# Four layer normalisations of an eight-block kernel: three dissolved into the stages that use them, one measured early

## What is computed

```python
def _layernorm(x, axis=-1, eps=1e-05):
    m = jnp.mean(x, axis=axis, keepdims=True)
    v = jnp.var(x, axis=axis, keepdims=True)
    return (x - m) / jnp.sqrt(v + eps)
...
    x = x + _L0_xattn_ref(_layernorm(x, axis=-1), ctx_2048, mask_1xSxS2_ff0, ...)   # grouped-query attention, 16 heads of 128
    x = x + _L0_ffn_ref(_layernorm(x, axis=-1), ...)    # silu gate, keep the 2 largest of every 4, down product
    x = x + _L1_xattn_ref(_layernorm(x, axis=-1), ctx_2048, ctx_2048, ...)          # linear attention with relu features
    x = x + _L1_ffn_ref(_layernorm(x, axis=-1), ...)    # 32 experts, top 6, shared expert
    x = x + _L2_xattn_ref(_layernorm(x, axis=-1), ctx_2048, ...)                    # cross attention, int8 rounding
    x = x + _L2_ffn_ref(_layernorm(x, axis=-1), ...)    # gelu gate in fp8
    x = x + _L3_xattn_ref(_layernorm(x, axis=-1), ctx_2048, ...)                    # windowed attention
    x = x + _L3_ffn_ref(_layernorm(x, axis=-1), ...)    # ternary weights
```

## Time and profile before

| what | us |
|---|---|
| median of 3 timed runs | 2308.69 (2306.54 to 2314.24) |
| the profiled execution, its own time | 2298.36 |
| its span, first to last instruction | 2296.4 |
| TensorE busy | 1939.6 (84%) |
| VectorE busy | 1378.1 (60%) |
| ScalarE busy | 1053.6 (46%) |
| GpSimd busy | 733.2 (32%) |

### The profile page before, as it was taken

One profiled execution on the slowest core, in us unless ns is written; L12 is line 12 of the kernel. 1 busy time (PEld: TensorE's weight loads), 2 busy tenths in 40 slices (PEclk: granted clock), 3 DMA queues, 4 the chain that ended last, 5 costly groups with the idle time before them and its releaser, 6 DMA issues. The chain is left out here.

```text
span 2296.4 us, 42607 instructions
## 1 busy us (share of the span) xinstructions
PE 1939.6 (84%) x11782; PEld 1303.3 (57%) x11798; DVE 1378.1 (60%) x3458; ACT 1053.6 (46%) x2770; POOL 733.2 (32%) x733
## 2 busy tenths in 40 slices
PE   6999999997998897776899999979856589888655
PEld 3666666664555565553566676635533357777432
DVE  5566565565776343343634343469879547777687
ACT  4554554453222221101244444367768417767576
...
GB/s 304 307 168 0 0 0 0 0 1 0 0 0 0 1 9 49 58 109 122 97 162 163 179 174 138 128 1 2 1 58 1 56 41 24 38 29 39 30 17 21
DMA packets 145575, 145.10 MB, mean 63 GB/s; under 512 B 49376, under 2 KB 133568, under 8 KB 145344
## 3 DMA queue, kind: packets, MB, share of 16 engines
...
## 5 line engine op out<-in xcount | busy, mean ns | idle before, releaser
L1582 POOL DMA_INDIRECT expert_sums<-moe_rows_in,moe_to x128 | 197.9, 1546 | 150.4 <-DMA expert_sums<-moe_rows_in,moe_to 82.1
L1655 PE MATMUL moe_gate<-moe_places,moe_xt 128*128 x512 | 175.9, 466 | 2.0 <-issue 1.9
L1845 DVE COPY moe_ht_e<-moe_turned 128x256 f32<-128x256 f32 x128 | 54.3, 424 | 202.7 <-PE moe_turned L1663 176.4
L624 ACT ACTIVATE ga_prob<-ga_score,ga_neg_max 128x128 f32<-128x128 f32 x256 | 99.5, 390 | 153.3 <-DVE ga_neg_max L508 153.3
L263 POOL TENSOR_TENSOR ga_q_inv<-ga_q_sum,half 128x4 f32<-128x4 f32 x64 | 64.4, 1006 | 313.4 <-DVE ga_q_sum L491 313.4
L2854 POOL TENSOR_TENSOR wa_low<-wa_low,wa_top 128x512 f32<-128x512 f32 x128 | 133.0, 1039 | 93.4 <-DVE wa_top L3058 92.7
L1089 POOL DMA_INDIRECT slot_x<-early x96 | 93.8, 977 | 136.0 <-DVE early L1082 107.6
L320 PE MATMUL ga_proj<-early,ga_xt 128*128 128x512 f32 x256 | 122.4, 601 | 3.6 <-ACT xnt L594 3.6
L3055 DVE SCALAR_TENSOR_TENSOR wa_low<-wa_score,early 128x512 f32<-128x512 f32 x128 | 87.7, 686 | 57.9 <-PE wa_score L2894 55.3
L391 PE MATMUL ga_summed<-ga_wo,ga_out_t 128*128 128x256 f32 x512 | 121.1, 379 | 0.7 <-ACT ga_out_t L632 0.7
L391 PEld LDWEIGHTS ga_summed<-ga_wo,ga_out_t 128*128 128x128 f32 x512 | 97.0, 190 | 40.2 <-issue 29.2
...
## 6 DMA issues: line engine op xcount, KB each, us to landing
moe_places<-in_L_ffn_packed SPq DMA_DIRECT2D x128, 608.0 KB
...
moe_rows_in<-slot_x SPq DMA_DIRECT2D x128, 134.5 KB
...
```

What stands on the lines that cost most here:

```text
L624: last = act.activation(prob[:, n % 2, part], score[:, n % 2, part], ACT.Exp, bias=neg_max[:, n % 2, h:h + 1], accum_out=total[:, n % 2, h ...
L1582: pool.indirect_dma_start(out=mem.sums[j % SUMS], out_offset=bass.IndirectOffsetOnAxis(ap=to[:, j:j + 1], axis=0), in_=y[:, j, :], in_offs ...
L1655: last = pe.matmul(both[j % 2][:, 0:2 * FE], xt[:, j % 2, c, :], packed[:, place, c * 2 * FE:(c + 1) * 2 * FE].rearrange("p a n -> p (a n) ...
```

## The change

Stages "ln1", "ln2" and "ln6" are gone, "ln5" is kept. A `RowsNorm` object for each of the four is handed to the stage before and the stage that uses it (`norm_next` and `norm`).

- The stage before computes variance, root and shift of tiles 0 to 11, whose sums are ready early; `gqa_attention` does it in its last pass, in three parts. The last four tiles are done at the start of the user.
- The user does the rows itself: norm by ScalarE, transposes by TensorE, copy by ScalarE. `sparse_ffn` does them one tile ahead in its loop, the last iteration is unrolled, and at its end it prepares the first four tiles of the linear attention. `linear_attention` does tiles 4 to 15 in its loop over tiles, through the free half of the value bank. `window_projections` makes the context's key product first and does the rows in groups of four.
- GpSimd's staging copies in `sparse_ffn` and `window_projections` are dropped.
- "ln5" is left with the variance of four tiles, the rows by VectorE, transposes in pairs of tiles and eight copies of 512 columns instead of 16 of 256.
- The opening of `gqa_attention` is put in another order: the first key, query and value products read `mem.ctxt` and `mem.xnt` directly, the keys go ahead of the rows, the queries' transposes use another bank (`summed`), the load of the second group of x is issued earlier, and the rows' norm is one slot earlier.

The stage "ln5" (VectorE), and the last pass of `gqa_attention` (GpSimd, then VectorE):

```diff
-                        last.then_inc(xn_ready.sem, 1)
+                norm.variance(dve, B - GROUP, B)
+                for t in range(B):
+                    if t == GROUP:
+                        norm.shifts(dve, 1, B - GROUP, B)
+                    if t == B - GROUP:
+                        dve.wait_ge(norm.shifted.sem, norm.shifted.at(1))
+                    if t >= GROUP:
+                        dve.wait_ge(row_turned.sem, row_turned.at((t - GROUP) // 2))
+                    dve.tensor_scalar(xn[:, t % GROUP, :], mem.x[:, t, :], norm.rstd[:, t:t + 1], norm.shift[:, t:t + 1],
+                                      ALU.mult, ALU.add).then_inc(row_normed.sem, 1)
...
+                    if isinstance(t, int) and t == B // 2 - 1 and n in (1, 3, 5):
+                        norm_next.root(pool, n // 2, n // 2 * GROUP, (n // 2 + 1) * GROUP)
...
-                    if early and n in (0, 2, 4):
+                    if early and n in (2, 4):
...
+                    if isinstance(t, int) and t == B // 2 - 1:
+                        if n in (0, 2, 4):
+                            dve.wait_ge(stat.sem, stat.at(t, -3))
+                            norm_next.variance(dve, n // 2 * GROUP, (n // 2 + 1) * GROUP)
+                        if n in (2, 4, 6):
+                            norm_next.shifts(dve, n // 2 - 1, (n // 2 - 1) * GROUP, n // 2 * GROUP)
```

The opening of `gqa_attention` on TensorE:

```diff
+                project_first(K_FIRST, mem.ctxt[:, :, 0:P], w.wk, mem.k_loaded, 2)
                 turn_rows(0)
-                project_first(K_FIRST, ct, w.wk, mem.k_loaded, 3, 0)
-                project_first(Q_FIRST, xt, w.wq[:, :, 0:G * D], mem.q_loaded[0], 2, 1)
+                pe.wait_ge(row_moved.sem, row_moved.at(0))
+                project_first(Q_FIRST, mem.xnt[:, :, 0:P], w.wq[:, :, 0:G * D], mem.q_loaded[0], 2)
                 turn_rows(1)
                 turn_rows(2)
-                project_first(V_FIRST, ct, w.wv, mem.v_loaded, 2, 0)
+                transpose_q(0, 0)
                 transpose_k(0, 0)
-                transpose_q(0, 0)
-                pe.wait_ge(row_moved.sem, row_moved.at(2))
+                project_first(V_FIRST, mem.ctxt[:, :, 0:P], w.wv, mem.v_loaded, 2)
+                pe.wait_ge(k_moved.sem, k_moved.at(0, 0))
```

`sparse_ffn` on GpSimd, TensorE, ScalarE (end) and VectorE:

```diff
-                with pool.Fori(0, B) as t:
-                    pool.wait_ge(gated.sem, gated.at(t, -1))
-                    pool.tensor_copy(xt[:, :, :], mem.xnt[:, :, bass.ds(t * P, P)]).then_inc(staged.sem, 1)
+                norm.root(pool, GROUPS - 1, B - GROUP, B)
+                norm_next.root(pool, 0, 0, B - GROUP)
...
+                def turn_row(t):
+                    pe.wait_ge(row_normed.sem, row_normed.at(t))
+                    for c in range(HC):
+                        last = pe.transpose(row_t[:, c * P:(c + 1) * P], xn[:, c * P:(c + 1) * P], mem.ident[:, :])
+                    last.then_inc(row_turned.sem, 1)
+
...
+                turn_row(0)
                 gate_up(0)
-                with pe.Fori(1, B) as t:
+                turn_row(1)
+                with pe.Fori(1, B - 1) as t:
                     gate_up(t)
+                    turn_row(t + 1)
                     turn_down(t - 1)
+                gate_up(B - 1)
+                turn_down(B - 2)
+                turn_ahead(0, row_t)
+                pe.wait_ge(silued.sem, silued.at(B - 1, 0))
+                turn_ahead(1, gate[0])
                 turn_down(B - 1)
...
+                silu(B - 1, 0)
+                sizes(B - 1, 0)
+                silu(B - 1, 1)
+                move(B - 2)
+                sizes(B - 1, 1)
+                for t in range(GROUP):
+                    norm_ahead(t)
+                move_ahead(0, row_t)
+                move_ahead(1, gate[0])
                 move(B - 1)
...
+                norm.variance(dve, B - GROUP, B)
+                norm.shifts(dve, GROUPS - 1, B - GROUP, B)
                 multiply(0)
                 sparsify(0)
-                with dve.Fori(1, B) as t:
+                with dve.Fori(1, B - 1) as t:
                     multiply(t)
                     sparsify(t)
                     update(t - 1)
+                dve.wait_ge(stat.sem, stat.at(B - 3))
+                norm_next.variance(dve, 0, B - GROUP)
+                multiply(B - 1)
+                norm_next.shifts(dve, 0, 0, B - GROUP)
+                sparsify(B - 1)
+                update(B - 2)
```

`linear_attention` on GpSimd, TensorE, ScalarE and VectorE:

```diff
+                norm.root(pool, 1, B - GROUP, B)
                 router.constants(pool)
...
-                pe.wait_ge(ready.sem, 4)
-                pe.wait_ge(route_loaded.sem, 16)
...
+                def turn_row(i):
+                    pe.wait_ge(row_normed.sem, row_normed.at(i))
+                    pe.wait_ge(v_moved.sem, v_moved.at(i))
+                    for c in range(HC):
+                        last = pe.transpose(value[:, H + c * P:H + (c + 1) * P], xn[:, i % 2, c * P:(c + 1) * P], mem.ident[:, :])
+                    last.then_inc(row_turned.sem, 1)
+
                 def features_values(t, j):
                     i = t * TG + j
                     behind(pe, v_moved, i - 1)
+                    behind(pe, row_moved, min(i, B - GROUP) - 1)
                     for c in range(HC):
...
+                    if t >= 1:
+                        pe.wait_ge(row_moved.sem, row_moved.at(t * TG - 1))
...
+                    if g == 0:
+                        pe.wait_ge(route_loaded.sem, 16)
                     if g >= 0:
                         router.logits(pe, g)
...
                         pair_up(t, j)
+                        if t < G - 1:
+                            turn_row(t * TG + j)
                         if j >= 1:
                             turn_mixed(t, j - 1)
...
-                        behind(act, summed, i - 1)
-                        act.activation(mixed_t[:, :, :].rearrange("p c s -> p (c s)"), turned[:, 0:H], ACT.Copy).then_inc(t_moved.sem, 1)
+                        if t < G - 1:
+                            if j == 0:
+                                norm_row(t * TG)
+                            move_row(t * TG + j)
+                            if j < TG - 1:
+                                norm_row(t * TG + j + 1)
+                        if j >= 1:
+                            move_mixed(t * TG + j - 1)
+                    move_mixed(t * TG + TG - 1)
...
+                norm.variance(dve, B - GROUP, B)
                 dve.wait_ge(mem.la_loaded.sem, 16 * mem.la_loads)
                 dve.wait_ge(ready.sem, 4)
+                norm.shifts(dve, 1, B - GROUP, B)
```

`cross_attention` and `gelu_ffn` on VectorE, `window_projections` on GpSimd, TensorE and ScalarE:

```diff
+                dve.wait_ge(counted.sem, counted.at(B - GROUP - 1))
+                norm_next.variance(dve, 0, B - GROUP)
                 round_mixed(LASTB)
                 count(LASTB - 1)
+                norm_next.shifts(dve, 0, 0, B - GROUP)
                 add(LASTB)
...
+                dve.wait_ge(stat.sem, stat.at(G - 2, TG - 1))
+                norm_next.variance(dve, 0, B - GROUP)
                 finish(G - 1)
...
-                    products = [[(w.wq[:, c, m * P:(m + 1) * P], sources[c]) for c in range(2 * HC)] for m in range(HC)]
-                    products += [[(w.wsk[:, c, :], sources[c]) for c in range(HC)], [(w.wk[:, c, :], sources[HC + c]) for c in range(HC)]]
+                    products = [[(w.wsk[:, c, :], sources[c]) for c in range(HC)]]
+                    products += [[(w.wq[:, c, m * P:(m + 1) * P], sources[c]) for c in range(2 * HC)] for m in range(HC)]
+                    products += [[(w.wk[:, c, :], sources[HC + c]) for c in range(HC)]]
                     for n, pairs in enumerate(products):
                         pe.wait_ge(moved.sem, moved.at(t, n - 2))
+                        if n == 1:
+                            if t == 0:
+                                turn_rows(0)
+                                turn_rows(1)
+                            pe.wait_ge(row_moved.sem, row_moved.at(2 * t + 1))
                         for c, (lhs, rhs) in enumerate(pairs):
...
+                        if t + 1 < B // TG and j % 2 == 1:
+                            turn_rows(2 * (t + 1) + j // 2)
...
+                for t in range(TG):
+                    norm_row(t)
...
+                        if t == 0 and n == 0:
+                            move_rows(0)
+                            move_rows(1)
+                    if t + 1 < B // TG:
+                        for k in range(TG):
+                            norm_row((t + 1) * TG + k)
+                        for k in range(2):
+                            move_rows(2 * (t + 1) + k)
```

289 lines of the change are left out of this document (173 added, 116 removed).

## The result

The changed kernel takes **2270.56 us** (median of 4 runs, 2263.65 to 2276.07) beside 2307.61 us for the kernel before in the same session: 37 us less, ratio 0.983 (95% interval 0.980 to 0.986). The forecast was 2286, so the sign was right and the gain was 1.7 times as large as the sum of -22.4. In two later sessions, on two other chips, the ratio was 0.979 (2219.6 us beside 2267.2, interval 0.977 to 0.981, and 2222.7 beside 2268.7, interval 0.975 to 0.983). These intervals overlap with the first one, so a better ratio there is likely and not shown. One execution of a later run (2409 us, a3_ln12) fell into a slower state of the chip and stands in no median and no interval here.

The account below looks back on a forecast made before the run. TensorE, busy 84% of the span, was taken as the bound, with idle holes around the normalisation stages. Terms summed to -22.4 us: 2276 from the profiled 2298.4, or 2286 by the timed median; range 2269 to 2303.

Parts of the forecast that it names:

- opening, up to the first scores: Kernel opening: first key projection needs only its load, query projection comes earlier; -3 us (-4.5 to 0).
- ln1, gap and low clock: Ahead of the sparse FFN: gap shrinks to one row's chain, 11.2 us, less 1.5 for low clock; -9.8 us.
- filling: Sparse FFN pipeline filling: tile 1's copy comes some 1.6 us later, about half swallowed; +0.8 us (0.6 to 1.6).
- rows in the sparse FFN: Inside the sparse FFN: two added transposes for each of tiles 1 to 15, 0.30 us each; +4.5 us (3.9 to 6.8).
- its end: Sparse FFN's end: 1.0 us VectorE delay against 1.0 us from added transposes keeping the clock up; 0 (-2 to +1).
- ln2: Ahead of the linear attention: stage removed, first projection starts at once; -14.3 us (-13 to -15.8, projections slow or fast).
- rows in the linear attention: Inside the linear attention: transposes plus about 0.25 us wait before the value product, 12 tiles; +5.4 us (3.1 to 7.8).
- ln6 and rows in the window projections: Window projections: first product starts with the stage, -8.0 us; later 24 transposes where TensorE is full, +3.3 us.
- Rival 1: Linear attention: VectorE's two 24.14 us waits go (-18, 2268 us, chance 0.08) or come a third time (+9, 2295, 0.05).
- Rival 2: Sparse FFN and linear attention: hand-overs cost 1.2 us or more a tile; 2308 to 2320 us, chance 0.10.
- Rival 3: Three dissolved normalisation stages: gaps close only by half, since weights or memory sets ended last; +16 us, 2302, chance 0.12.
- Rival 4: Last attention pass: GpSimd's roots delay the query root in three slots; at most +3.5 us, no chance given.

Follow-up runs that it names:

- a3_ln12: Kernel before with only the new opening and the first and second normalisation stages dissolved; 2231.6 us, ratio 0.9861 to before.
- b1_before: The kernel before, unchanged, profiled again on the third chip; 2269.2 us.
- a1_opening: Kernel before with only the new opening of the first attention, all other stages old; 2258.6 us, ratio 0.9955 to before.
- b2_rows_late: Changed kernel with the rows' norm put back one slot later in the first attention's first pass; 2220.6 us, ratio 0.9802 to before.
- b4_fill: Changed kernel with ScalarE copying the second row before the second size operation at the sparse FFN's start; 2224.2 us, ratio 0.9825 to before.
- c4_dummy: Changed kernel with three extra 512-column products, result unused, ahead of the sparse FFN's last down product; 2223.6 us, ratio 0.9791 to before.
- b3_rows_early: Changed kernel with each row's transposes ahead of the pair products in the linear attention; 2215.5 us, ratio 0.9789 to before.
- c3_tail: Changed kernel with row transposes ahead of pair products and two next-group query projections in the linear attention's group-end waits; 2204.0 us, ratio 0.971 to before.
- d1_before_tail: Kernel before with only the next group's first two query projections moved into the linear attention's group-end waits; 2294.7 us, ratio 0.9944 to before.
- a4_all: The whole change run again on the second chip, against the kernel before; 2219.6 us, ratio 0.979.

## Why the prediction was right or wrong

| term | predicted | by the traces |
|---|---|---|
| opening, up to the first scores | -3 | -3.1 |
| norm of rows a slot earlier, direct reads, in the first pass | not priced | -9.5 |
| variance in the last attention pass | +1.5 | 0 to +1.7 |
| ln1, gap and low clock | -9.8 | -11.3 + 1.3 = -10.0 |
| filling | +0.8 | 0 |
| rows in the sparse FFN | +4.5 | +2.4 |
| its end | 0 | 0 |
| ln2 | -14.3 | -14.4 - 1.4 = -15.8 (the clock part is 2.7 to 3.1 in four other profiles) |
| rows in the linear attention | +5.4 | +6.0 at full clock; -1 to +6 as it ran |
| cross attention, ln5 | +0.5, -3.3 | +0.2, -3.4 |
| ln6 and rows in the window projections | -8.0 + 3.3 | -6.3 to -7.2 |

The right column, with the linear attention as it ran, adds to -38 to -47; the timed change on the second and third chip was -48 and -46, on the first -37. The terms are differences between the profiles of before and of changed kernels. The prediction's own bounds add to -35.9 on the good side and -4.0 on the bad one, not to -38 and -5: even with every term at its best the sum did not reach the measured gain.

One agreement is luck. The prediction has 2276 us for the profiled execution, and the profiled execution took 2276.07. In that profile the unpriced 9.5 us of the first pass are there, and the linear attention with its stall came out 12.3 us longer instead of the 5.4 of the sum; the two errors, with the smaller ones of the table and the drift of untouched stages (experts +3.3, window attention +4.1), cancel.

**Opening: the failed step.** The first scores come 3.11 us earlier, the forecast. But the prediction ended there. The section on the change lists "the rows' norm is one slot earlier", and the sum has no term for it, which puts it at nothing without a reason. The kernel before showed the place in one view: TensorE waited 9.4 us for `ga_xn` and `xnt` between 22 and 100 us. The prediction's rows of the opening end at its first product. The runs show 9.5 us in place of nothing: from the first scores to those of the eleventh slot it is 89.2 us in the kernel before (90.6 in b1_before) and 79.7 in all twelve profiles with the whole new opening, a1_opening among them, where nothing else is changed. With the norm put back (b2_rows_late) only 3.1 of the 9.5 are left, so by this one trace the slot is worth 6.4. At 9.5 us this is the largest error of the sum, over a quarter of the whole gain.

**ln1.** The chain of one row was right: the stage opens at 522.1 and the gate starts 1.6 us later (1.9 predicted), with the low clock for its first four instructions (3.26 us, 1.3 more). The filling was over-charged: from first gate to first down product it is 19.73 us against 18.47, and those 1.26 us are the cold start alone; the delay of tile 1 is swallowed whole, and b4_fill shows that making its wait shorter gives nothing. The cold start is no sure cost of the change: in b1_before, with the old stage, the first four instructions took 3.65 us as well. A row's two transposes cost 0.17 us a tile (11.93 against 11.76), not 0.30. The steady tile of the changed kernel shows why:

```profile
697.00 0.38 PE L726 MATMUL sf_row_t<-ident,sf_xn 128*128 128x128 f32 x2
697.22 1.04 PE L752 MATMUL sf_turned<-ident,sf_kept 128*128 128x128 f32 x8
698.51 3.72 PE L758 MATMUL sf_down<-sf_wd,sf_ht 128*128 128x256 f32 x16 [0.25 <-ACT sf_ht L795]
```

The row's transposes hold TensorE for 0.22 us, without the gap that was feared, and the wait ahead of the down product is 0.25 instead of the 0.30 of the earlier trace rows.

**The end of the sparse FFN.** The eight added transposes did not keep the clock up: 1.97 and 5.77 us for the last transposes and down product, as in the earlier trace rows. Over all profiles the down product took 4.76 to 5.83 us without and 4.34 to 5.86 with these transposes, and 3.69 in the two kernels with the extra products. The term 0 came out since the charged delay was not there either (the wait for VectorE is 3.13 us behind 0.87 us of added transposes, together the 4.00 of before). c4_dummy shows that products in that rest bring 1.09 and 3.69 us. The Trainium skill, "TensorE: Matmul & The Clock Gate", Part 4: PE-mode transpose, says that a transpose does not count for the clock as a product does; the trace agrees so far as it goes, with 0.87 us of transposes ahead 5.77 us, with 2.74 us of products 3.69. As many transposes in place of the products were not run, so that it is the kind of instruction and not the filled rest is not shown.

**ln2** is the most exact of the large terms: gap -14.4 against -14.3. Of the two cases named for the first projections the better came, 3.67 us for eight in every profile without the stage; with it they took 5.08 us in one profile and 6.37 to 6.74 in four.

**Rows in the linear attention.** The wait was the predicted one, in nine places, 3.5 us in all; the longest is over the 0.5 us that the prediction names as a sign of being wrong:

```profile
810.16 0.42 PE L1289 MATMUL la_value<-ident,la_xn 128*128 128x128 f32 x2
811.14 1.10 PE L1297 MATMUL la_value<-la_wv,ctxt 128*128 128x256 f32 x4 [0.56 <-ACT xnt L1388]
```

Yet the stage took 225.8 to 233.9 us in eight profiles with rows (b3_rows_early among them), and 227.1 to 227.9 in three without. The 5.4 us are not visible in the total, because the clock hides them. At full clock the stage is 197.9 to 198.0 us without rows and 203.6 to 204.6 with them, so the rows cost **6.0 us** and the term was right. What differs beside it is the time that TensorE was busy at the low level: 58 to 60 us in the three profiles without rows, 60 to 61 in three of the seven with them and 42 to 49 in the other four. In the three the stage is 6 us longer, as forecast; in the four the clock gives back 5 to 8 us. Whether the rows have a part in that is open.

What the prediction took as full ("15.00 of 15.00") was a stretch without a group's end; over a whole group the kernel before is busy 53.84 of 57.15 us at a granted clock of 0.86 (b1_before):

```profile
817.66:874.81 57.15, 53.84 (x243) 37.80 (x242) 28.08 (x85) 11.64 (x20) 7.10 (x7) 0.86 0.04 15
```

So "TensorE is full there" was read in too narrow a window. It did not mis-size this term, since the rows stand between the group's ends, but it hid what c3_tail and d1_before_tail found: 18.6 and 12.9 us less with the rests covered (the first with the rows' transposes moved as well).

**ln5** -3.4 (from 17.4 to 14.0 us between the cross attention and the gelu FFN) against -3.3.

**ln6.** The opening of the window projections is the predicted one to a few tenths of a microsecond (a4_all, ScalarE, then TensorE):

```profile
1740.79 0.31 ACT L3330 ACTIVATE tw_ones<-ident 128x128 f32<-128x128 f32 x1 [3.12 <-PEq L32]
```

```profile
1741.05 3.60 PE L2845 MATMUL wp_proj<-ctxt,early 128*128 128x512 f32 x4 [4.50 <-ACTq L2859]
1744.44 1.14 PE L2825 MATMUL wp_turned<-ident,wp_xn 128*128 128x128 f32 x8
1746.31 1.98 PE L2845 MATMUL wp_proj<-ctxt,early 128*128 128x512 f32 x4 [0.74 <-ACT xnt L2871]
```

The first product starts with the stage at low clock, the next one 5.3 us later (5.5 us into the stage), at full clock. The charged 0.9 us for the clock did not come here; it did in the profiles in which this stage takes 63.1 us (the transposes ahead then take 1.91 us instead of 1.14), five of nine. The three later batches of transposes cost 1.7 us in both cases instead of 3.3. Together that is -1.6 to -2.5 on the sum.

**Rivals.** Rival 1 (the stall in the linear attention goes or grows) did not happen: on the first chip the stall was there twice with 24.1 us as before, and none of the twelve profiles on the second and third chip has it. Rival 2 is out (0.17 us a tile in the sparse FFN, 0.5 in the linear attention, where it needed 1.2). Rival 3 is out: the gaps of ln1, ln2 and ln6 closed to 3.6, 1.7 and 4.5 us. Rival 4 stayed inside its range.

**The stall and the smaller gain on the first chip.** VectorE's largest waits from 720 to 1000 us, changed kernel, first chip:

```profile
DVE early L1083 <- remote: 48.2, 2, 24.1
```

The same reduction in the changed kernel on the second chip waits for its scores only:

```profile
862.88 0.29 DVE L1083 TENSOR_REDUCE early<-la_scores 128x4 f32<-128x128 f32 x1 [13.10 <-PE la_scores L1076]
```

The stall was the same 24.1 us before and after the earlier trace rows. Where it does not show, the stage is 227.9 us before and 225.9 to 233.9 after; where it does, 248.2 and 260.5. At full clock that is 198.0 and 220.2 us before, 204.0 (mean of seven) and 225.9 after: the stall costs 22 us both times, and the change does not make it dearer. The rest of the stage's growth on the first chip is the clock: TensorE was busy at the low level for 69.1 us there, 56.1 before. That is one profile of each kernel. Whether the gain of the first chip (-37) is really smaller than the others' (-46, -48) the overlapping intervals leave open.
